# Blocks 1 to 3 of a gated feed-forward kernel: the first gate and up products of a slab as seven half-size products

## The reference

```python
xn = _layernorm(x, axis=-1)
# "attn": the half of each row with the smallest |silu(gate)| is zeroed
s = silu(einsum('bsh,ih->bsi', xn, w_gate))
_, idx = top_k(-abs(s), int(0.5 * I))
s = s.at[rows, idx].set(0.0)
s = einsum('bsi,hi->bsh', s * einsum('bsh,ih->bsi', xn, w_up), w_down)
# "ffn": the same without the zeroing, with other weights
g = silu((silu(xt @ W_gate.T) * (xt @ W_up.T)) @ W_down.T)
out = x + s * g
```

## Time and profile before

| | us |
|---|---|
| median of 3 runs | 2833.18 (2832.59 to 2833.91) |
| profiled execution, its span | 2830.1 |
| TensorE busy | 2822.0 |
| VectorE busy | 1890.2 |
| ScalarE busy | 1220.6 |
| GpSimd busy | 657.5 |

### The profile page before, as it was taken

How to read it: one execution, slowest core, us unless ns; L and a number is a source line. 1 busy time by engine, 2 the same in 40 slices (tenths; PEclk the granted TensorE clock), 3 DMA queues, 4 the chain that set the end, 5 groups by cost and what they waited for, 6 DMA issues and landing times.

```text
span 2830.1 us, 31490 instructions
## 1 busy us (share of the span) xinstructions
PE 2822.0 (100%) x12564; PEld 2343.8 (83%) x12564; DVE 1890.2 (67%) x2522; ACT 1220.6 (43%) x1224; POOL 657.5 (23%) x281
## 2 busy tenths in 40 slices
PE   9999999999999999999999999999999999999999
PEld 7888888888888888888888888888888888888887
DVE  5126999989211689998732178999872207899981
ACT  4336988233222577711122257771112226776110
POOL 6665443024544100000054400000005440000000
PEclk9999999999999999999999999999999999999999
DMA  6667888579422455556532255555653225555564
GB/s 258 235 247 276 291 290 285 193 277 314 148 97 95 168 193 193 193 194 251 191 127 96 95 179 193 193 193 193 254 183 127 96 93 190 193 193 193 193 227 174
DMA packets 100034, 549.98 MB, mean 194 GB/s; under 512 B 10992, under 2 KB 10992, under 8 KB 53104
## 3 DMA queue, kind: packets, MB, share of 16 engines
q1 hardware_dynamic: 99952, 548.97, 54.8%
HBM read 449.31 MB, written 99.61 MB: 194 GB/s over the span
## 4 chain that ended last, share of the span: by engine, by line
PE 99%; DVE 0%; ACT 0%; DMA 0%; SPq 0%; POOL 0%; issue 0%; DVEq 0%
PE ps L433 33%; PE ps L604 11%; PE ps L602 11%; PE ps L603 11%; PE ps L573 11%; PE ps L576 11%; PE ps L574 11%; DMA w_raw<-w_a 0%; PE ps L442 0%; DVE prods L986 0%; ACT prods L683 0%; POOL w_split L859 0%; ACT w_split L650 0%; SPq L363 0%; DVE hid_buf L1242 0%
## 5 line engine op out<-in xcount | busy, mean ns | idle before, releaser
L859 POOL TENSOR_TENSOR w_split<-w_raw,w_split 128x1024 fp32r<-128x1024 f32 (+1 forms) x242 | 577.0, 2388 | 1687.1 <-ACT w_split L650 1524.3
L433 PE MATMUL ps<-w_split,hid_ring 128*128 128x512 f32 x4096 | 931.6, 389 | 0.0
L433 PEld LDWEIGHTS ps<-w_split,hid_ring 128*128 128x128 f32 x4096 | 768.1, 188 | 162.3 <-issue 2.9
L1000 DVE TENSOR_SCALAR_CACHE_REDUCE ranks<-key_buf,cand 128x2752 int16<-128x2752 f32 x248 | 762.9, 3076 | 5.8
L673 ACT ACTIVATE signs_row<-key_buf,cand 128x2752 bf16<-128x2752 f32 x248 | 642.3, 2590 | 191.0 <-DVE cand L1009 181.6
L604 PE MATMUL ps<-xnT,w_split 128*128 128x512 f32 x1376 | 535.3, 389 | 0.0
L603 PE MATMUL ps<-xnT,w_split 128*128 128x512 f32 x1376 | 535.3, 389 | 0.0
L602 PE MATMUL ps<-xnT,w_split 128*128 128x512 f32 x1376 | 535.3, 389 | 0.0
L1030 DVE TENSOR_TENSOR prods<-ps,key_buf 128x512 f32<-128x512 f32 (+1 forms) x96 | 61.1, 636 | 701.5 <-ACT key_buf L714 701.4
L573 PE MATMUL ps<-w_split,xnT 128*128 128x512 f32 (+1 forms) x1376 | 528.8, 384 | 0.3 <-POOL w_split L859 0.3
L574 PE MATMUL ps<-w_split,xnT 128*128 128x512 f32 (+1 forms) x1376 | 528.3, 384 | 0.0
(11 more groups left out here) (101 smaller groups left out, 1398.4 us busy)
## 6 DMA issues: line engine op xcount, KB each, us to landing
...
w_raw<-w_a SPq DMA_DIRECT2D x160, 512.0 KB, 3.5
...
w_raw<-w_b SPq DMA_DIRECT2D x42, 512.0 KB, 4.5
w_stage_raw<-wd_b SPq DMA_DIRECT2D x22, 512.0 KB, 4.9
w_raw<-wd_a SPq DMA_DIRECT2D x22, 512.0 KB, 5.2
prods<-x SPq DMA_DIRECT2D x16, 512.0 KB, 5.9
```

What stands on the lines that cost most here:

```text
L433: ins = pe.matmul(ps[:, 2 * t + half, :], h, w[:, half * TB:(half + 1) * TB], start=(first and n == 0), stop=last and stop)
L859: pool.tensor_tensor(w_lo[q][:, 0:w], w_raw[q][:, 0:w], w_hi[q][:, 0:w].bitcast(F32), ALU.subtract).then_inc(lo_ready, 1)
L1000: dve.tensor_scalar(ranks[:, :], keys[:, t, :], cand_f[:, t:t + 1], 0.0, ALU.is_lt, ALU.add, accum_out=counts[:, t:t + 1]).then_inc(sel_st ...
```

## The change

In blocks 1 to 3 the five full slabs of A are computed by Strassen's scheme in Winograd's form. A slab's product is a 2 by 2 block product: tokens in two halves of 256, input features in two halves (even and odd chunks), output in gate and up. Seven products of half size in each dimension (`P4, P1, P6, P5, P7, P2, P3`) replace eight. Their token sides are four halves of xn and four sums (`s_sum` on GpSimd, split into high and low parts by `s_hi` on ScalarE and `s_lo` on VectorE); their weight sides are three of the stored quarters and four sums T1 to T4, which VectorE makes in block 0 from A's raw tiles (`t_unit`, 20 units) and SyncE writes to DRAM (`t_dram`); slab 0's are made from a second load of its tiles.

A tile of the new kind holds two chunks by 512 columns, so a slab has 14 tiles with 12 matmuls each, where it had 8 with 24. They go through six places: the ring's four and two more (`w_extra`). Every one is loaded raw, its high part made by ScalarE (`hi_w`), its low part by GpSimd (`low_w`). Products are added up partly in PSUM (P7 onto P6's bank, P2 onto P1's, P3 onto P5's) and partly by VectorE and ScalarE through `keys` and `prods` (`w_slab`, `w_finish`, `w_step`). The last 192 features are computed as before, in other banks. Block 0's A is as before but for `t_unit`; 11 instead of 22 FFN-down tiles are split ahead (`STAGED`, one in four A tiles, three staging places), and the other 11 are split in FFN-down of block 0. The outputs of a block are added between low parts of the next block's tiles 2 and 3. Stages B, FFN-down and attention-down of blocks 1 to 3 are unchanged.

```diff
+SEVEN = 7
+W_SLAB = 2 * SEVEN
+W_REST = NS * W_SLAB
+W_TILES = W_REST + KC // 2
+W_RING = RING + 2
+W_TURNS = W_TILES // W_RING
...
+P4, P1, P6, P5, P7, P2, P3 = range(SEVEN)
...
-STAGES = 4
-SPLITS_0 = TILES - NJ
+STAGES = 3
+STAGED = 11
...
+UNITS = []
+for slab in range(1, NS):
+    UNITS += [(slab, 0), (slab, 1), (0, slab - 1), (slab, 2), (slab, 3)]
+T_BUFS = 3
...
+                def t_unit(unit):
+                    n = UNITS.index(unit)
+                    tb = t_buf[n % T_BUFS]
+                    s, j = unit
+                    steps, reads = t_steps_before(unit), t_reads_before(unit)
+                    if n >= T_BUFS:
+                        dve.wait_ge(t_stored[n % T_BUFS], 16 * (n // T_BUFS))
+                    if s == 0:
+                        dve.wait_ge(t_landed, 32 * (j + 1))
+                        gates, ups = (tb[:, 0, :], tb[:, 2, :]), (tb[:, 1, :], tb[:, 3, :])
+                    else:
+                        q = [(s * KC + 2 * j + half) % RING for half in range(2)]
+                        gates, ups = [w_raw[q[h]][:, 0:SLAB] for h in range(2)], [w_raw[q[h]][:, SLAB:2 * SLAB] for h in range(2)]
+                        dve.wait_ge(landed[q[0]], (s * KC + 2 * j) // RING * 16 + 16)
+                    dve.tensor_tensor(tb[:, T1, :], ups[0], gates[0], ALU.subtract).then_inc(t_step, 1)
+                    if s == 0:
+                        dve.wait_ge(t_step, steps + 1)
+                        dve.tensor_tensor(tb[:, T3, :], ups[1], ups[0], ALU.subtract).then_inc(t_read, 1)
+                        dve.wait_ge(t_read, reads + 1)
+                    else:
+                        dve.tensor_copy(tb[:, T3, :], ups[0]).then_inc(t_read, 1)
+                        dve.wait_ge(landed[q[1]], (s * KC + 2 * j + 1) // RING * 16 + 16)
+                        dve.wait_ge(t_read, reads + 1)
+                        dve.tensor_tensor(tb[:, T3, :], ups[1], tb[:, T3, :], ALU.subtract).then_inc(t_step, 1)
+                    dve.wait_ge(t_step, steps + 1)
+                    dve.tensor_tensor(tb[:, T2, :], ups[1], tb[:, T1, :], ALU.subtract).then_inc(t_step, 1)
+                    dve.wait_ge(t_step, steps + (2 if s == 0 else 3))
+                    dve.tensor_tensor(tb[:, T4, :], gates[1], tb[:, T2, :], ALU.subtract).then_inc(t_read, 1)
...
+                def w_finish(s):
+                    cols = slice(s * SLAB, (s + 1) * SLAB)
+                    dve.wait_ge(tiles_done, w_done(b, s * W_SLAB + 2 * P3 + 1))
+                    for t in range(STAGE):
+                        dve.tensor_tensor(prods[:, t, cols], ps[:, 6 + t, :], prods[:, t, cols], ALU.add).then_inc(w_c12, 1)
+                    dve.wait_ge(w_g1, w_events(b, s) + 2)
+                    dve.wait_ge(w_c12, w_events(b, s) + 2)
+                    for t in range(STAGE):
+                        dve.tensor_tensor(prods[:, t, cols], prods[:, t, cols], keys[:, t, cols], ALU.mult).then_inc(w_prod, 1)
+                    w_keys(s, range(STAGE))
+                def w_slab(s):
+                    cols = slice(s * SLAB, (s + 1) * SLAB)
+                    a = s * W_SLAB
+                    if s == 0:
+                        s_lo(1)
+                    dve.wait_ge(tiles_done, w_done(b, a + 2 * P6 + 1))
+                    if s == 0:
+                        dve.wait_ge(s_ready, (b - 1) * 4 + 2)
+                    for t in range(STAGE):
+                        dve.wait_ge(w_e1, w_events(b, s) - STAGE + (t + 1))
+                        dve.tensor_tensor(prods[:, t, cols], ps[:, 4 + t, :], keys[:, t, cols], ALU.add).then_inc(w_u2, 1)
+                    if s == 0:
+                        s_lo(2)
+                        s_lo(3)
+                    dve.wait_ge(tiles_done, w_done(b, a + 2 * P7 + 1))
+                    for t in range(STAGE):
+                        dve.tensor_tensor(keys[:, STAGE + t, cols], ps[:, 4 + t, :], keys[:, t, cols], ALU.add).then_inc(w_v, 1)
+                    dve.wait_ge(w_e5, w_events(b, s))
+                    for t in range(STAGE):
+                        dve.wait_ge(w_v, w_events(b, s) + 2 - STAGE + (t + 1))
+                        dve.tensor_tensor(prods[:, STAGE + t, cols], keys[:, STAGE + t, cols], prods[:, STAGE + t, cols], ALU.add).then_inc(w_c22, 1)
+                    for t in range(STAGE):
+                        dve.wait_ge(w_c22, w_events(b, s) - STAGE + (t + 1))
+                        dve.tensor_tensor(keys[:, STAGE + t, cols], ps[:, t, :], keys[:, STAGE + t, cols], ALU.add).then_inc(w_c21, 1)
+                    for t in range(STAGE):
+                        dve.wait_ge(w_g2, w_events(b, s) - STAGE + (t + 1))
+                        dve.tensor_tensor(prods[:, STAGE + t, cols], prods[:, STAGE + t, cols], keys[:, STAGE + t, cols], ALU.mult).then_inc(w_prod, 1)
+                    w_keys(s, range(STAGE, NT))
...
+                def w_product(p, s):
...
+                    for pair in range(2):
+                        a = s * W_SLAB + 2 * p + pair
+                        w_weights(a)
+                        if p == P4:
+                            pe.wait_ge(xn_ready, parts_before(b) + (4 if pair == 0 else 7))
+                        elif p == P1 and pair == 1:
+                            pe.wait_ge(xn_ready, parts_before(b) + KC)
+                        hi_w, lo_w, _ = w_place(a)
+                        for t in range(STAGE):
+                            for n in range(2):
+                                cols = slice(n * SLAB, (n + 1) * SLAB)
+                                for part, w in ((0, hi_w), (0, lo_w), (1, hi_w)):
+                                    ins = pe.matmul(ps[:, W_BANK[p] + t, :], tokens_of(p, pair, n, part, t), w[:, cols],
+                                                    start=(p in (P4, P1, P6, P5) and pair == 0 and n == 0 and part == 0 and w is hi_w),
+                                                    stop=(pair == 1 and n == 1 and part == 1),
+                                                    skip_group_check=p in (P7, P2, P3))
+                        ins.then_inc(tiles_done, 1)
...
+                    elif i == 2 * P2 + 1:
+                        for t in range(STAGE):
+                            act.wait_ge(w_c21, w_events(b, s) + 2 - STAGE + (t + 1))
+                            act.activation(keys[:, STAGE + t, cols], keys[:, STAGE + t, cols], ACT.Silu).then_inc(w_g2, 1)
...
+            def low_w(b, a):
+                high, lo, raw = w_place(a)
+                pool.wait_ge(hi_ready, w_splits_before(b, a) + 1)
+                pool.tensor_tensor(lo, raw, high.bitcast(F32), ALU.subtract).then_inc(lo_ready, 1)
```

More of the change, by code:

```diff
@@ new lines, in _ @@
+            for m in range(TILES):
+                if m == 0:
+                    pool.wait_ge(xn_normed, NORMS_0)
+                if m == AD0:
+                    pool.wait_ge(masked, NT)
+                if stage_at(m) is not None and m >= FIRST_TILES:
+                    low_stage(stage_at(m))
+                if m >= TILES - 4:
+                    s_sum(1, m - (TILES - 4))
+                if is_split(0, m):
+                    low(0, m)
+                if m == FIRST_TILES - 1:
+                    low_stage(0)
@@ L902, in _ @@
             dve.sem_inc(signs_used, 1)
+            dve.sem_inc(w_c21, 2)
+            dve.sem_inc(w_v, 2)
+            dve.sem_inc(w_c12, 2)
             dve.wait_ge(consts, 2)
```

505 lines of the change are left out of this document (406 added, 99 removed).

## The result

| | before | after |
|---|---|---|
| median, us | 2833.2 (2832.6 to 2833.9) | 2793.1 (2792.5 to 2793.6) |
| profiled span | 2830.1 | 2791.5 |
| TensorE busy, matmuls | 2822.0, 12564 | 2751.0, 12204 |
| TensorE not busy | 8.1 | 40.5 |

A forecast was written before the change was run, and what follows sets the result against it. TensorE was taken to bound the kernel, by matmul count and its waits. From 2833.2 us, -81.6 + 16.8 + 14.5 + 13.0 + 2.5 = -34.8 gave 2798.4 us; range 2776 to 2828, with 2786 to 2818 at 0.52.

The forecast's parts named there:

- The 81.6 us: Slabs of blocks 1 to 3: 168 matmuls replace 192, 5.44 us less per slab, 81.6 us less in all.
- The steady state: Inside a slab of A, blocks 1 to 3: loads, high parts and low parts keep ahead of TensorE; cost 0.
- Block 0's A: Stage A of block 0: VectorE's added units and traffic of about 307 GB/s stay hidden; cost 0.
- that the port costs little: Rival: few collisions in block 0 and cheap boundaries, losses of about 22 us, 2774 us; chance 0.13 for 2786 and below.
- that GpSimd has no reserve: Rival: in slabs GpSimd needs 38.4 of 38.1 us, costing 57 us, 2855 us; chance 0.11, partly so (2818 us) 0.20.
- The walk inside a slab: From tile 10 to low part 15: GpSimd idles 3.8 us, TensorE's lead falls to 2.4 us and grows back; cost 0.
- FFN-down: 16.8 said: Block 0's FFN-down: 11 low parts on GpSimd delay VectorE 18.5 us, transposes end at 610.6 us; +16.8 us (0 to 24.6).
- of the delay only 1.8 is covered: Last step for block 0's FFN-down: VectorE's smallest lead in attention-down, 1.8 us, taken off its 18.5 us delay.
- Boundary: 14.5 said: Block 0 to 1: low part 18 late by 3.5 us, banks freed late, then GpSimd's queue; +14.5 us (6 to 20).
- Starts of blocks 2 and 3: 6.5 said: Output sums alternate with low parts on GpSimd, so tile 4 starts late: 6.5 us each, +13.0 us (8 to 20).
- End of A: 2.5 said: End of stage A: rest tiles wait for the last slab's w_c12 sums, 0.8 us each, +2.5 us (0 to 9).
- The clock: Rival: TensorE runs at 1.2 GHz after waits, 14 to 27 us on top, 2812 to 2825 us; within a chance of 0.20.

The follow-up runs named there:

- the runs of two more operations: Kernel after with two VectorE bit operations repeated per slab in blocks 1 to 3: 2808.9 us; not in the last slab: 2792.4; in the last slab alone: 2803.1.
- six more: Kernel after with six bit operations more per slab in blocks 1 to 3: 2893.7 us, ratio 1.0211 to the kernel before.
- the two turns of the experiment: Two bit operations added per slab to the kernel after, ahead of the last slab's w_c12 sums too: 2808.9 us; in the last slab alone: 2803.1 us.

## Why the prediction was right, and where not

**Right.** The 81.6 us, from the count of matmuls and the slab spacing. The steady state at no cost, with slabs of 38.1 us. Where the rest would be lost: FFN-down of block 0 by turns between GpSimd and VectorE, and the boundary behind it and the starts of blocks 2 and 3 by GpSimd's queue and these turns. Block 0's A: 1.0 us where 0 was said, with 301 to 311 GB/s where 307 was. Rivals: that the port costs little fell (two bit operations of 0.42 us took 5.17), that GpSimd has no reserve fell with the slab spacing and with the runs of two more operations, though with six more it is VectorE's sums that TensorE waits for.

**The walk inside a slab** came out at 0 as said, but one part of it doesn't fit. It had GpSimd idle for 3.8 us ahead of low part 15, with 36.3 us of work in 38.1: together more than a slab, so the lead could not have grown back. Low part 15 did begin 8.8 us after tile 10, but GpSimd was at work until 0.6 us before it. Over four slabs of block 2 it was busy for 38.1, 37.5, 34.6 and 37.5 us.

**FFN-down: 16.8 said, 12.4 found.** The walk of VectorE's list was good: the last transposes of this stage, said to end at 610.6, are

```profile
601.32 8.25 DVE L1636 STREAM_TRANSPOSE key_buf<-prods 32x320 f32<-32x320 f32 x16
```

and so end at 609.6, 17.5 us later than before. The step that was mis-sized is the last one, "of the delay only 1.8 is covered". TensorE starts attention-down only 13.4 us later (611.8 instead of 598.4), so 4.1 us were covered. What it waits for is ScalarE's queue, which takes the high parts of the first two transposed tiles and then the SiLU that frees a bank. Now, then the SiLU before:

```profile
609.61 1.15 ACT L968 ACTIVATE hid_ring<-key_buf 128x512 fp32r<-128x512 f32 x2 [11.00 <-DVE key_buf L1636]
610.66 3.75 ACT L1151 ACTIVATE hid_buf<-ps 128x1024 f32<-128x1024 f32 x4
```
```profile
596.41 3.98 ACT L796 ACTIVATE hid_buf<-ps 128x1024 f32<-128x1024 f32 x4 [1.07 <-PE ps L442]
```

From the last transpose to TensorE it is now 2.2 us (609.6 to 611.8), before it was 6.3 (592.1 to 598.4), since the SiLU waited there for TensorE's own last matmuls. That difference is the lead of 4.1 us at this place. I had taken the smallest lead of the next stage, 1.8 us at tile 9, for it. Besides, 2.2 of the 12.4 us are not waits but slower matmuls.

**Boundary: 14.5 said, 15.2 found** (6.3 + 9.4, less 0.5 for the end of A), but for other reasons than the sum had. Waits are 9.1 us: low part 18 is 1.6 us late, not 3.5 (the two times from which this was taken, 699.4 and 696.3, are 3.1 apart), the banks come free 1.15 late, the norm 1.05, tiles 3 and 4 2.55 and 2.71. The other 6.1 are slower matmuls, behind the wait of 6.41 us and behind the last two.

**Starts of blocks 2 and 3: 6.5 said, 6.9 found**, 5.75 of it waits. Tile 4 begins 16.6 us after the block's first matmul ("about 17"), and the wait for `xn` lies inside the delay, as said.

**End of A: 2.5 said, 0.5 found**, in block 1 alone. Here I was lucky in the direction: the place holds by less than the two turns of the experiment.

**The clock.** This rival I priced at 14 to 27 us and left out of the sum; the runs show 10.6 us. So the sum of 46.8 us of waits was too high by 14 (32.4 found) and had nothing for the clock, and the two errors nearly met. That the forecast came within 5.3 us is partly luck.

The rule of the Trainium skill that was weighed (in "SBUF — State Buffer", Who interferes with whom) is borne out for the scan of 16-bit data, which no row of before had shown: GpSimd's low part beside it takes 7.14 us instead of 2.4, while the scan keeps its 5.89.

```profile
586.15 5.89 DVE L1606 TENSOR_TENSOR_SCAN ranks<-ranks 128x2752 int16<-128x2752 int16 x1
```
```profile
587.05 7.14 POOL L1218 TENSOR_TENSOR w_split<-w_raw,w_split 128x1024 fp32r<-128x1024 f32 x1 [3.45 <-ACT w_split L943]
```

It ends 2.15 us after the scan does, little less than a whole low part: as the lengths read, it did its work only then. So it is GpSimd that waits for what has started on VectorE, and VectorE's next operation (a hidden low part of 2.78 us instead of 0.69) that pays.
